# Batched feature interaction: stores of eight batches from three staging slots in place of four batches from six

## What is computed

```python
bilinear = jnp.einsum('bie,ied->bid', feature, weight)
out = jnp.einsum('bid,bjd->bij', bilinear, feature)
```

## Time and profile before

| what | us |
|---|---|
| median of three runs | 1340.6 |
| the profiled execution, its own time | 1343.22 |
| its span, from first to last instruction | 1341.4 |
| from the span's start to the first matmul of scores (first products, weights) | 49.1 |
| scores of block 0 | 75.4 |
| scores of blocks 1 to 14, each with the next block's transposes and products | 1138.3 in all |
| scores of block 15, which has no block after it | 64.5 |
| from the last matmul to the end | 14.0 |

### The profile page before, as it was taken

The page is one execution under the profiler, slowest core; times in us unless marked ns, Lnnn a source line. Parts: engine busy times, 40 slices in busy tenths (PEclk is TensorE's granted clock), DMA queues, the critical chain, the costliest instruction groups (busy, mean ns, idle before and its releaser), DMA issues.

```text
span 1341.4 us, 57339 instructions
## 1 busy us (share of the span) xinstructions
PE 1200.1 (89%) x24384; PEld 1024.5 (76%) x24384; DVE 926.0 (69%) x1792; ACT 1059.4 (79%) x1185; POOL 387.0 (29%) x631
## 2 busy tenths in 40 slices
PE   5899998998988998998989999899889999989974
PEld 4788777887777876887878877788677887778853
DVE  0477676686766776767777776777767777767884
ACT  4798787887788876987779978798777888879853
POOL 2133232232322332323232322322223333232321
PEclk9999999999999999999999999999999999999998
DMA  9799999999999999999999999999999999999888
GB/s 239 215 351 351 339 328 351 329 327 354 328 332 324 323 345 332 348 319 328 355 333 339 330 335 354 334 350 324 340 322 312 351 342 331 343 331 347 296 287 293
DMA packets 286621, 439.71 MB, mean 328 GB/s; under 512 B 60064, under 2 KB 258720, under 8 KB 286368
## 3 DMA queue, kind: packets, MB, share of 16 engines
q1 hardware_dynamic: 234400, 317.95, 67.4%
q0 software_dynamic: 51968, 118.10, 29.4%
HBM read 108.13 MB, written 327.68 MB: 325 GB/s over the span
## 4 chain that ended last, share of the span: by engine, by line
PE 38%; DMA 30%; SPq 15%; ACT 9%; issue 7%; DVE 1%; ACTq 0%; POOLq 0%; POOL 0%; DVEq 0%
DMA out_dram<-staging 27%; PE ps L282 24%; SPq L183 15%; PE ps L251 7%; ACT staging L312 7%; PE ps L264 6%; DMA x<-feature_dram 3%; ACT bl L332 2%; ACT xt L324 1%; DVE win L359 0%; DVE staging L312 0%; DVE win L367 0%; DVE win L366 0%; ACTq L311 0%; SPq L153 0%
## 5 line engine op out<-in xcount | busy, mean ns | idle before, releaser
L282 PE MATMUL ps<-win,bl 64*64 64x200 f32 x16384 | 845.6, 340 | 75.5 <-ACT staging L312 45.5
L282 PEld LDWEIGHTS ps<-win,bl 64*64 64x64 f32 x16384 | 672.9, 175 | 175.1 <-issue 70.6
L312 ACT COPY staging<-ps 128x800 f32<-128x800 f32 x768 | 630.9, 867 | 208.1 <-DMA out_dram<-staging 91.7
L227 POOL DMA_DIRECT2D out_dram<-staging x512 | 301.5, 589 | 888.6 <-ACT staging L312 626.9
L312 DVE COPY staging<-ps 128x800 f32<-128x800 f32 x256 | 253.5, 990 | 255.6 <-PE ps L282 224.3
L359 DVE COPY win<-xt 128x400 f32<-128x400 f32 x512 | 282.0, 551 | 127.1 <-PE ps L282 63.0
L332 ACT COPY bl<-ps 128x1024 f32<-128x1024 f32 (+1 forms) x208 | 306.7, 1475 | 30.9 <-PE ps L264 29.2
L251 PE MATMUL ps<-ident,x 128*128 128x128 f32 x1600 | 223.2, 282 | 41.3 <-DMA x<-feature_dram 19.5
L251 PEld LDWEIGHTS ps<-ident,x 128*128 128x128 f32 x1600 | 174.1, 142 | 95.0 <-issue 83.2
L264 PE MATMUL ps<-xt,w 64*64 64x128 f32 x6400 | 232.3, 273 | 10.4 <-issue 8.5
L324 ACT COPY xt<-ps 128x1024 f32<-128x1024 f32 (+1 forms) x208 | 210.7, 1013 | 32.1 <-PE ps L251 31.9
(11 more groups left out here) (2 smaller groups left out, 0.2 us busy)
## 6 DMA issues: line engine op xcount, KB each, us to landing
out_dram<-staging SPq DMA_DIRECT2D x1536, 200.0 KB, 5.9
x<-feature_dram POOLq DMA_DIRECT2D x96, 1024.0 KB, 9.4
out_dram<-staging POOLq DMA_DIRECT2D x512, 25.0 KB, 5.7
x<-feature_dram POOLq DMA_DIRECT2D x16, 256.0 KB, 6.1
w<-weight_dram SPq DMA_DIRECT2D x24, 128.0 KB, 8.0
w<-weight_dram SPq DMA_DIRECT2D x2, 64.0 KB, 6.2
```

Source lines behind the costliest of these rows:

```text
L227: nc.gpsimd.dma_start(out_v[3 * Z:FH, b:b + R, :], staging[3:4 * C:4, slot].rearrange("p b h j -> p b (h j)")).then_inc(rest_written[slot] ...
L282: last = nc.tensor.matmul(tile[64 * g:64 * g + 64, h ^ g, F * b:F * (b + 1)], lines_of_bl(n, h, g, R * ORDER[s // 2] + r), win[64 * h:64 * ...
L312: copy(staging[:, slot, PB * (s % 2):PB * (s % 2 + 1)].rearrange("p b h j -> p h b j"), tile_of("s", n, s)[:, :, 0:PB * F].rearrange("p h ...
```

## The change

Slots hold eight batches (`OCT`), and there are three of them, so that `staging` keeps its size. SP waits for four sets and issues three DMAs of 32 partitions x 8 batches; POOL does the same with its four partitions. The order of quads becomes 0, 1, 4, 5, 2, 3, 6, 7 (the same from 8 and 16), so that the two quads of one store are neighbours in DRAM. The groups keep their cells, but a group's two quads are no longer neighbours in the order: `quads_before(u)` says how many quads must be done before its room is free, and transposes and products move one set later. For odd blocks `store_bl` walks its elements in another order, with the 4 x 2 places of a group innermost (16 and 256 bytes apart in `bl`, 512 and 2048 bytes apart in PSUM).

```diff
-    OSLOTS = 6
+    OCT = 8
+    OSLOTS = 3
...
-    ORDER = [8 * a + 4 * g + i for a in range(CELLS // 8) for i in range(4) for g in range(2)]
-    ORDER = ORDER[:LINES - 1] + list(range(LINES - 1, CELLS))
+    ORDER = [8 * a + i for a in range(LINES // 8) for i in (0, 1, 4, 5, 2, 3, 6, 7)]
+    ORDER += list(range(LINES - 1, CELLS))
...
-    transposed_at = {60 * u // NG + 1: u for u in range(NG)}
+    def quads_before(u):
+
+        return max(ORDER.index(t) for t in cells_of(u)) + 1
+
+    transposed_at = {60 * u // NG + 2: u for u in range(NG)}
     weighed_at = {s + 3: u for s, u in transposed_at.items()}
...
-        staging = sbuf("staging", [128, OSLOTS, R, 2, F])
+        staging = sbuf("staging", [128, OSLOTS, OCT, 2, F])
...
             def store(q):
                 slot = q % OSLOTS
-                n, k = q // QUADS, ORDER[q % QUADS]
-                b = n * NB + R * k
-                wait_staged(sp, 2 * q)
-                wait_staged(sp, 2 * q + 1)
+                n, first = q // (QUADS // 2), 2 * (q % (QUADS // 2))
+                for s in range(OCT // PB):
+                    wait_staged(sp, OCT // PB * q + s)
+                assert ORDER[first + 1] == ORDER[first] + 1
+                b = n * NB + R * ORDER[first]
                 for z in range(3):
-                    sp.dma_start(out_v[Z * z:Z * (z + 1), b:b + R, :],
+                    sp.dma_start(out_v[Z * z:Z * (z + 1), b:b + OCT, :],
                                  staging[z:128:4, slot].rearrange("p b h j -> p b (h j)")
                                  ).then_inc(out_written[slot], 16)
...
-                    if s % 2:
-                        store_rest(n * QUADS + s // 2)
+                    if PB * (s + 1) % OCT == 0:
+                        store_rest((n * SETS_B + s) * PB // OCT)
...
-            slot = at // 2 % OSLOTS
+            slot = at * PB // OCT % OSLOTS
             engine.wait_ge(scores_done, at + 1)
-            used = at // 2 // OSLOTS
+            used = at * PB // OCT // OSLOTS
...
-                    act.wait_ge(own_filled, (n - 1) * QUADS + min(2 * u + 2, LINES))
+                    act.wait_ge(own_filled, (n - 1) * QUADS + quads_before(u))
...
-                    act.wait_ge(scores_done, (n - 1) * SETS_B + 2 * min(2 * u + 2, LINES))
-                nc.scalar.copy(group_of_bl(n, u),
-                               bilinear_tile(n, u).rearrange("p g c (a v) -> p g c v a", a=4)
-                               ).then_inc(bl_stored, 1)
+                    act.wait_ge(scores_done, (n - 1) * SETS_B + 2 * quads_before(u))
+                at = "p g c v a -> p g c v a" if n % 2 == 0 else "p g c v a -> p v a g c"
+                weighed = bilinear_tile(n, u).rearrange("p g c (a v) -> p g c v a", a=4)
+                nc.scalar.copy(group_of_bl(n, u).rearrange(at), weighed.rearrange(at)).then_inc(bl_stored, 1)
```

More of the change, by code:

```diff
@@ L47, in feature_interaction, with cells_of @@
     out_v = out.rearrange("b (m h) j -> m b (h j)", h=2)
-    transposed_at = {60 * u // NG + 1: u for u in range(NG)}
+    def cells_of(u):
+        return [8 * (u // 4) + u % 4, 8 * (u // 4) + u % 4 + 4] if u < NG - 1 else [LINES - 1]
+    def quads_before(u):
+        return max(ORDER.index(t) for t in cells_of(u)) + 1
+    transposed_at = {60 * u // NG + 2: u for u in range(NG)}
     weighed_at = {s + 3: u for s, u in transposed_at.items()}
-    assert all(s >= 2 * min(2 * u + 1, LINES - 1) + 1 for s, u in weighed_at.items())
+    assert all(s >= 2 * quads_before(u) - 1 for s, u in weighed_at.items())
     assert max(weighed_at) < SETS_B
@@ L70, in staged_by_dve @@
         return s % 4 == 3
-    def cells_of(u):
-        return ORDER[2 * u:2 * u + 2] if u < NG - 1 else [LINES - 1]
     ctx = ExitStack()
@@ L188, in _ @@
                 load_w(u)
-            for n in range(BLOCKS):
-                for s in range(SETS_B):
-                    if s % 2:
-                        store(n * QUADS + s // 2)
+            for q in range(BLOCKS * QUADS // 2):
+                store(q)
             for slot in range(OSLOTS):
-                uses = (BLOCKS * QUADS - slot + OSLOTS - 1) // OSLOTS
+                uses = (BLOCKS * QUADS // 2 - slot + OSLOTS - 1) // OSLOTS
                 sp.wait_ge(out_written[slot], 48 * uses)
@@ L223, in store_rest @@
                 slot = q % OSLOTS
[L224 to L227, removed]
+                b = q // (QUADS // 2) * NB + R * ORDER[2 * (q % (QUADS // 2))]
+                for s in range(OCT // PB):
+                    wait_staged(pool, OCT // PB * q + s)
+                nc.gpsimd.dma_start(out_v[3 * Z:FH, b:b + OCT, :],
                                     staging[3:4 * C:4, slot].rearrange("p b h j -> p b (h j)")
@@ L311, in stage @@
                 engine.wait_ge(rest_written[slot], 16 * used)
-            copy(staging[:, slot, PB * (s % 2):PB * (s % 2 + 1)].rearrange("p b h j -> p h b j"),
+            copy(staging[:, slot, PB * s % OCT:PB * s % OCT + PB].rearrange("p b h j -> p h b j"),
                  tile_of("s", n, s)[:, :, 0:PB * F].rearrange("p h (b j) -> p h b j", j=F)
```

## The result

The changed kernel takes 1307.03 us (median of four runs, 1305.47 to 1310.32) against 1341.26; the ratio is 0.9745, interval 0.9728 to 0.9761. It is faster by 34 us; 77 were forecast. Its profiled execution has a span of 1304.5 us and a granted clock of 0.987.

The account below looks back on a forecast made before the run. SP's store issue was taken as the fullest station in a ring with DMA, PE and ACT close behind. 49.1 + 74.5 + 14 x 77 + 63 = 1264.6 us of span, forecast 1264 us; own range 1202 to 1308, 8-in-10 range 1215 to 1365.

Parts of the forecast that it names:

- Fewer issues: SP's queue, each block: 48 stores instead of 96, at 0.80 us with the gap, 38 us instead of 73.7.
- the 73.7 us before: SP in blocks 1 to 14 before the change: 0.77 us a store, 73.7 of 81.3 us a block, 91% occupied.
- DMA at 72.5 us: Next fullest station once SP is relieved: a block's 27.03 MB at 373 GB/s take 72.5 us.
- 77 a block: Blocks 1 to 14: 76.3 us, plus 0.5 for the end of a block and the transposes' move, rounded to 77.
- the rival of the full engines: DMA engines already full at 341 GB/s; relieving SP changes nothing before block 15, 1326 us. Chance 0.12.
- PE at 70.9 us: PE's time a block: 13 rounds of 5.45 us from one bilinear product to the next are 70.9 us.
- The ring's surcharge: Time a block that the ring of stations adds to 72.5 us: 0 to 7.6 us, middle taken, giving 76.3.
- Starved slots: Three slots, each refilled only when all of eight batches have landed, starve the queue: 1408 us, mostly nearer 1340 to 1400. Chance 0.22.
- The order of the odd copy: ACT's odd-block copies of products: 1.0 to 2.0 us each, full gain worth 4 us, none taken.
- Block 15: Last block: SP's bound goes, 57 us taken; with the tail 63 instead of 78.5, a gain of 15.5.
- The tail: After block 15: 0.1 + 1.3 + 2.9 + 1.65 = 6 us for the last store.
- The signs I named: Right if issues take 0.6 to 0.9 us, SP's waits exceed 500, blocks 74 to 80, last block with tail about 63.

Follow-up runs that it names:

- the transfers alone: Changed kernel with PE, ACT and DVE doing nothing; SP and POOL issue the same stores and loads, stores carry zeros: 1193.5 us.
- a stream of matmuls: The changed kernel's transfers with nothing else but unsynchronized 16-column matmuls on PE, 48768 instructions in all: 1862 us, the matmuls outlasting the transfers.
- the copies above: The changed kernel's transfers with only unsynchronized copies beside them, 1185 on ACT and 1536 on DVE: 1839 us, the parts not ending together.

## Why the prediction was wrong

The direction was right, and so was the first half of the mechanism: fewer stores free the way out. What comes next was priced wrongly. By the terms of the sum, forecast and measured span: start 49.1 and 49.2; block 0, 74.5 and 76.0; blocks 1 to 14, 14 x 77 = 1078 and 1109.4; block 15 with its tail 63 and 69.85; in all 1264.6 and 1304.5. Of the 40 us missed, 31 lie in blocks 1 to 14.

- **Fewer issues: right.** 48 stores at 0.82 us are 39.4 us a block where 38 were forecast; the weight loads were the right row for it, and undoing the stores alone undid everything. Less sure is the reading of the 73.7 us before as SP's own time: an issue also takes in what holds it up (1.22 us at the median in the transfers alone).
- **DMA at 72.5 us, and 77 a block from it: this step failed.** "The next is DMA at 72.5" took the 373 GB/s of ten microseconds for what the engines can hold through a block. As the transfers' own rate it is right, 72.2 us alone. Beside a stream of matmuls it is 79.3, and in the kernel without products, where compute has slack, 77.5. The trace had a warning: block 1 as a whole, share 1.01 and 341 GB/s. I had it in the rival of the full engines and gave it 0.12. That 27.03 MB at 341 GB/s are 79.3 us, and 79.25 was measured, is partly luck: a rate over a whole block is the block's bytes over its time, and block 1 still had 96 stores to issue. Nor are 79.25 us a floor of the transfers: 351 GB/s and 77.35 us were reached with more slots and smaller loads.
The Trainium skill (SBUF — State Buffer, Who interferes with whom) says that DMA never contends with a compute engine. ACT's copies bear that out, 375 GB/s beside them. The transfers do slow beside the stream of matmuls, to 337; whether the two meet in SBUF, which is what the page speaks of, or on the way of the code no run shows.
- **PE at 70.9 us, taken as fixed: also wrong.** Blocks 1 to 14 with two of three stores left out:

```profile
120.15:1128.27 1008.12, 1002.13 (x21343) 885.41 (x21337) 813.11 (x1569) 925.03 (x1037) 210.21 (x320) 1.00 0.57 195
```

For the same matmuls PE is busy 1002 us there and 1042 in the changed kernel, 71.6 and 74.4 us a block. Of the 101 us between the two, 40 are longer work of PE (some 10 of them, by estimate, from the granted clock, 0.99 for 1.00) and the rest is PE standing: for ACT's staging 35.0 us, for nothing that the profile names 25.5 (2.3 in the run above). So the slowing goes both ways, and the chain after the change, 66% PE, fits that better than a bound by transfers alone. The shares of the two are not separated.
- **The ring's surcharge: the wrong reading of a bound.** I took the middle of 0 and 7.6 us. With 72.5 as the floor it came out as 6.75, nearly all of it. It is mostly not what I thought, stalls in a ring of few slots: four slots gave back 0.8 us and half-size loads 1.1. The other 5 us, by which compute and transfers together are slower than either alone, were not a term of the sum at all.
- **Starved slots: rightly held less likely.** ACT's wait for slots fell from 69.1 to 33.8 us, and the landing moved from 5.9 to 6.3.
- **The order of the odd copy: right,** worth nothing; the copy stays at 2.0 us. By the rule of the Trainium skill (SBUF — State Buffer, Door 1: The DMA port swizzle) on 16-byte lines it would; the trace agrees, 2.0 us at a step of 16 bytes as of 512, though the wider reads of PSUM could hold it there too.
- **Block 15: half right.** SP's bound went, and the block took 59.0 us where 57 were forecast. The tail was the larger miss, 10.8 instead of 6: SP was still issuing the last seven stores, of 400 KB each, 4.7 us after the last matmul. With two of three stores left out, block and tail are

```profile
1128.27:1186.23 57.96, 50.29 (x1031) 34.70 (x1024) 54.35 (x108) 36.65 (x49) 9.49 (x16) 1.00 0.36 128
1186.23:1191.50 5.27, 0.00 (x1) 0.00 (x0) 0.99 (x1) 0.32 (x1) 0.59 (x1) 0.78 0.50 175
```

so that the block hardly hangs on the DMA rate (58.0 us at 128 GB/s, DVE busy 54.4), and the tail does hang on the stores.
- **The signs I named** read rightly: SP's waits over 500 us, issues of 0.6 to 0.9 us, a landing under 9 us. "340 to 365 GB/s" allowed 343, and blocks of 74 to 80 us allowed 79.25: the own range of the forecast held the result at its upper edge, its point did not. One sign failed: the last block with its tail fell to 69.85 us, not to about 63.

## What to carry to other kernels

A queue that only issues has no row of busy time: take its count, subtract its waits from the stretch, and see whether what is left per issue fits the fastest issue; here 0.77 us times 96 filled 91% of the block, and halving the number of stores was worth 2.5%, with an issue that did not grow with its runs. What is left per issue above the fastest one can be the station behind it, holding the issue up. Before a relief is priced, price the next station in the state in which it will work: the best ten microseconds are only its upper limit, and a rate over a whole block only repeats the block's time. Where two stations seem equal, run each alone before adding buffers: here each alone took 72 us a block and both together 79, and buffers gave back less than 2 of the 7.

## What the runs showed of the hardware that was not expected

- An issue on SP's queue takes 0.597 us at the fastest and 0.62 at the median with 128 and with 256 runs, and 0.618 at the fastest with 512. In the transfers alone, with three stores of eight batches in flight, its median is 1.22.
- Transfers alone carry 368 GB/s with three stores of eight batches in flight and 342 with two; the matmul stream costs about as much as the missing third store.
- DVE's copies, made without a pause, hold up POOL's DMA: in the first 500 us shown for the copies above, POOL stands in a single DMA and nothing at all is moved. The Trainium skill (SBUF — State Buffer, Who interferes with whom) says that a DVE copy in a mode that uses the port pair shared with GpSimd blocks GpSimd's making of descriptors; the standstill agrees, 0 GB/s over 500 us, but no row shows in which mode the copies ran.
- The weight loads of L286 read `bl` 512 bytes apart in even blocks and side by side in odd ones; one takes 214 and 133 ns at the median, and PE's weight loads are busy 68.0 and 60.4 us a block. Even blocks are the longer ones, 80.7 to 77.8 us, and 74.0 to 70.0 with two of three stores left out, where PE is busy 99.4% of the time.
